# Two-layer RWKV and mixture-of-experts network on one core: dense experts' first units moved into the first layer's last tile, its first tiles reordered, and the low halves of the squared relus subtracted on VectorE

## The reference, cut to what matters

```python
h = W_E[x] * 16
xn = layernorm(layernorm(h))                   # h is normalized twice
w, k, v, r = -exp(xn @ Ww.T), xn @ Wk.T, xn @ Wv.T, sigmoid(xn @ Wr.T)
# along each sequence: num = decay*num + exp(w+k)*v ; den = decay*den + exp(w+k)
x2 = x1 + (r * num / (den + 1e-8)) @ Wo.T
kk = square(relu(layernorm(x2) @ Wkey.T))      # 1024 wide
h = h + x2 + sigmoid(layernorm(x2) @ Wrec.T) * (kk @ Wval.T)
xf = layernorm(h)
logits = xf @ Wrt + br                         # router of 8 experts, top 2, softmax
h = h + sum_e weight_e * (gelu(xf @ W1[e] + b1[e]) @ W2[e] + b2[e])   # 8 dense experts, 256 -> 1024 -> 256
# then the second layer: WKV attention, causal attention, 4 experts
```

## Time and profile before

| | |
|---|---|
| median of 3 runs | 3027.48 us (3025.65 to 3029.61) |
| profiled execution, its own time | 3026.94 us |
| its span in the profile | 3024.9 us |
| PE (TensorE matmul) busy | 2725.5 us, 90% |
| VectorE (DVE) busy | 1906.0 us, 63% |
| ScalarE (ACT) busy | 1842.6 us, 61% |
| GpSimd (POOL) busy | 391.2 us, 13% |
| mean granted TensorE clock | 0.979 |

### The profile page before, as it was taken

The page is one execution under the profiler, slowest core; times in us unless marked ns, Lnnn a source line. Parts: engine busy times, 40 slices in busy tenths (PEclk is TensorE's granted clock), DMA queues, the critical chain, the costliest instruction groups (busy, mean ns, idle before and its releaser), DMA issues.

```text
span 3024.9 us, 55642 instructions
## 1 busy us (share of the span) xinstructions
PE 2725.5 (90%) x22016; PEld 1819.0 (60%) x22016; DVE 1906.0 (63%) x4021; ACT 1842.6 (61%) x2877; POOL 391.2 (13%) x462
## 2 busy tenths in 40 slices
PE   3989877998999999999999999999999998998889
PEld 1555554565665566657665766566656665663665
DVE  5767736757666665666566665666565657656664
ACT  3666645655766566666665766576657665665644
POOL 5666530000000000100010001000100010011000
PEclk8999988999999999999999999999999999999999
DMA  1000008832122222222222222222222221110002
GB/s 64 22 21 20 21 13 309 286 119 78 63 74 96 77 74 71 88 80 76 76 89 86 76 67 89 81 76 76 90 80 76 74 77 63 71 57 27 27 24 79
DMA packets 59742, 235.66 MB, mean 78 GB/s; under 512 B 6585, under 2 KB 25073, under 8 KB 40689
## 3 DMA queue, kind: packets, MB, share of 16 engines
q1 hardware_dynamic: 57968, 228.14, 21.6%
q0 software_dynamic: 1536, 4.20, 0.5%
HBM read 200.57 MB, written 31.72 MB: 77 GB/s over the span
## 4 chain that ended last, share of the span: by engine, by line
PE 51%; DVE 16%; ACT 10%; issue 4%; DMA 2%; POOL 2%; SPq 0%; ACTq 0%; DVEq 0%
PE c_up L2303 15%; PE c_down L2318 14%; PE c_up L2053 8%; ACT c_g L1571 3%; PE c_down L2375 2%; DVE c_lo L1957 2%; DMA c_room<-in_WB 2%; PE c_front L2062 1%; PE c_front L2075 1%; DVE c_mx L1821 1%; PE c_front L2187 1%; DVE c_room L1739 1%; PE c_front L2053 1%; PE c_front L2191 1%; DVE h L1947 1%
## 5 line engine op out<-in xcount | busy, mean ns | idle before, releaser
L2303 PE MATMUL c_up<-c_xT,c_ring 128*128 128x512 bf16 x3072 | 743.2, 380 | 32.3 <-ACT c_g L1571 13.4
L2318 PE MATMUL c_down<-c_ring,c_hi 128*128 128x256 bf16 x4096 | 699.9, 274 | 21.4 <-DVE c_lo L1957 8.9
L1957 DVE TENSOR_TENSOR c_lo<-c_g,c_hi 128x512 bf16<-128x512 f32 x720 | 481.5, 685 | 308.3 <-ACT c_hi L1573 291.2
L1571 ACT ACTIVATE c_g<-c_up,b 128x512 f32<-128x512 f32 x512 | 350.3, 684 | 473.6 <-PE c_up L2303 458.2
L2318 PE MATMUL c_down<-c_ring,c_lo 128*128 128x256 bf16 x2048 | 560.3, 274 | 0.0
L2318 PEld LDWEIGHTS c_down<-c_ring,c_hi 128*128 128x128 bf16 x4096 | 394.2, 98 | 145.9 <-issue 30.0
L2303 PEld LDWEIGHTS c_up<-c_xT,c_ring 128*128 128x128 bf16 x3072 | 292.6, 98 | 312.6 <-ACT c_g L1571 21.8
L1573 ACT ACTIVATE c_hi<-c_g 128x512 bf16<-128x512 f32 x688 | 433.3, 630 | 21.7
L1393 POOL TENSOR_TENSOR c_xlo<-c_room,c_xhi 128x512 bf16<-128x512 f32 x48 | 54.8, 1157 | 1504.4 <-ACT c_xhi L1418 1504.4
L2318 PEld LDWEIGHTS c_down<-c_ring,c_lo 128*128 128x128 bf16 x2048 | 201.0, 98 | 24.0
L1571 ACT ACTIVATE c_g<-c_up 128x512 f32<-128x512 f32 x176 | 104.7, 595 | 179.7 <-PE c_up L2053 178.3
(11 more groups left out here) (353 smaller groups left out, 5018.6 us busy)
## 6 DMA issues: line engine op xcount, KB each, us to landing
c_ring<-kept_dense SPq DMA_DIRECT2D x112, 1024.0 KB, 4.8
c_ring<-kept_experts SPq DMA_DIRECT2D x63, 512.0 KB, 3.4
c_room<-in_WB SPq DMA_DIRECT2D x16, 1024.0 KB, 6.9
kept_dense<-c_ring SPq DMA_DIRECT2D x16, 1024.0 KB, 4.8
c_ring<-kept_experts SPq DMA_DIRECT2D x28, 384.0 KB, 3.4
kept_experts<-c_room SPq DMA_DIRECT2D x9, 512.0 KB, 4.5
c_xT<-kept_xT SPq DMA_DIRECT2D x8, 512.0 KB, 5.1
out<-h SPq DMA_DIRECT2D x8, 512.0 KB, 6.9
```

The lines of the kernel that those rows point to most:

```text
L1571: act.activation(g[:, h % 4, :], ub[n % 2][:, :], ACT.Gelu, bias=bias).then_inc(g_ready.sem, 1)
L1957: dve.tensor_tensor(lo14[:, a, :], g[:, h % 4, :], hi14[:, a, :], ALU.subtract).then_inc(lo_ready.sem, 1)
L2303: last = pe.matmul(ub[n % 2][:, :], r[:, wp, o + q * P:o + (q + 1) * P], xT[:, xp, q, :], start=(m == 0 and q == 0), stop=(m == 2 and q == ...
L2318: m = pe.matmul(bank, (hi14, lo14)[xp][:, a, s * P:(s + 1) * P], r[:, wp, o + KC * P:o + CHUNK], start=(k == 0 and n == 0 and s % 2 == 0), ...
```

## The change

Five things:

- **The experts' start moves into `phase_a`.** In the last tiles SP loads the first four weight pieces and tile 0's `xT`, ACT and VectorE split the first two (`wp0`, `wp1`), and PE and ACT do the units U0 to U4 (gelu of U0 to U3) (`up`, `up4`, order `ORDER_END`). For that, buffers of the two blocks are shared (`ring01`, `room0`, `xT`, `g`, `ub`). The block no longer waits for the last store to land; SP waits for it at the start of the next block. The router's maxima and softmax and some memsets go to later units (`ROUTER_AT`), so the exponential now stands between gelus.
- **The low halves of the squared relus** go from POOL to VectorE, one token later (`kl0` to `kl3`).
- **The order of the steady tiles**: `bx` after `c1`; `e0` on VectorE between the statistics of the second norm and its application (`c0n`).
- **The order of the first tiles** (`ORDER_FILL`), the constants `lc` last; POOL's masks go to the second block.
- **The loop over tiles 1 to 5** (`Fori`) is written out.

```diff
-ORDER_A = ("c0 bx b0 e0 d0 dx ag k0 b1 e1 c1 sm z0 k1 b2 c2 tr z0x c3 zx0 a0 c4 a0p z1 z1x c5 zx1 an l0 l1 c6 a1 c6p "
-           "dr lc l2 l3 l4 l5 l6").split()
+ORDER_A = ("c0 b0 e0 c0n d0 dx ag k0 b1 e1 c1 bx sm z0 k1 b2 c2 tr kl0 z0x c3 zx0 kl1 a0 c4 kl2 a0p "
+           "z1 z1x c5 zx1 an kl3 wp0 l0 l1 c6 a1 c6p wp1 dr l2 l3 l4 l5 l6 lc").split()
+ORDER_END = "up d0 dx up4 dr".split()
+ORDER_FILL = "ag bx b0 e0 a0 k0 b1 e1 a0p z0 k1 an b2 tr a1 z0x zx0 z1 z1x zx1".split()
...
-        fb = [x.enter_context(nc.psum_tensor(f"a_front{k}", [P, TT], F32)) for k in range(4)]
+        fb = c.ub + [x.enter_context(nc.psum_tensor(f"a_front{k}", [P, TT], F32)) for k in (2, 3)]
...
+        emb, xn = (c.ring01[0][:, j, :].bitcast(F32) for j in range(2))
+        x2, xn2 = (c.ring01[1][:, j, :].bitcast(F32) for j in range(2))
+        x1 = c.g[:, 0:2, :].rearrange("p k n -> p (k n)")
+        yf = c.g[:, 2:4, :]
...
+        ek, ev, num, den = (c.room0[:, j * KC * TT:(j + 1) * KC * TT].rearrange("p (k n) -> p k n", k=KC) for j in range(4))
+        tr = c.xT[:, :, :, :].rearrange("p a k n -> p (a k n)").bitcast(F32).rearrange("p (k n) -> p k n", k=KC)
...
-        def run(eng, A, B, C, D, L):
+        def run(eng, A, B, C, D, L, ahead):
 
             braid(A(0), L)
-            braid(A(1), B(0))
+            braid(A(1), B(0), order=ORDER_FILL)
             braid(A(2), B(1), C(0))
-            with eng.Fori(1, TILES - 2) as t:
+            for t in range(1, TILES - 2):
                 braid(A(t + 2), B(t + 1), C(t), D(t - 1))
             braid(B(TILES - 1), C(TILES - 2), D(TILES - 3))
-            braid(C(TILES - 1), D(TILES - 2))
-            braid(D(TILES - 1))
+            braid(C(TILES - 1), D(TILES - 2), ahead)
+            braid(D(TILES - 1), ahead, order=ORDER_END)
 
         block = x.enter_context(nc.Block())
 
...
-            with sp.Fori(0, TILES) as t:
+            for t in range(TILES):
+                if t == TILES - 2:
+
+                    sp.wait_ge(z_ready.sem, z_ready.at(TILES - 1))
+                    sp.wait_ge(xm_kept.sem, xm_kept.at(t, 0))
+                    sp.dma_start(c.xT[:, :, :, :], c.xd[0, :, :, :, :]).then_inc(c.xT_in.sem, 16)
+                    for p in range(2):
+                        sp.dma_start(c.room0[:, p * PIECE:(p + 1) * PIECE], c.i["WB"][p, :, :]).then_inc(c.loaded[p].sem, 16)
+                if t == TILES - 1:
+                    for q in range(2):
+                        sp.wait_ge(c.split, 2 * (q + 1))
+                        sp.dma_start(c.room0[:, q * PIECE:(q + 1) * PIECE], c.i["WB"][q + 2, :, :]
+                                     ).then_inc(c.loaded[q].sem, 16)
                 sp.wait_ge(xm_lo.sem, xm_lo.at(t))
                 for j, part in enumerate((c.xT_hi, c.xT_lo)):
                     sp.dma_start(c.xd[bass.ds(t, 1), :, j, :, :].rearrange("g p k n -> (g p) k n"),
                                  part[:, :].rearrange("p (k n) -> p k n", k=KC)[:, :, bass.ds(t * TT, TT)]
                                  ).then_inc(xm_kept.sem, 16)
             sp.wait_ge(s_b2, 16 * len(BIAS))
-            sp.wait_ge(xm_kept.sem, 32 * TILES)
-
         @block.gpsimd
         def _(pool):
...
-                def low(*ks):
-                    def f():
-                        for k in ks:
-                            pool.wait_ge(sq_ready.sem, sq_ready.at(t, k + 1))
-                            pool.wait_ge(k_hi.sem, k_hi.at(t, k + 1))
-                            pool.tensor_tensor(klo[:, k, :], sq[:, k % 2, :], khi[:, k, :],
-                                               ALU.subtract).then_inc(k_lo.sem, 1)
-                    return f
-
                 def b6():
                     rstd(bmv, brs, b_var, b_rstd, b_pool, t, 1)
-                return {"c0": b0, "c1": b1, "c2": low(0, 1), "sm": summed, "c3": low(2, 3), "c4": low(4, 5), "c5": low(6, 7),
-                        "c6p": b6}
-            run(pool, stage_a, stage_b, stage_c, lambda t: {}, {"lc": masks})
+                return {"c0": b0, "c1": b1, "sm": summed, "c6p": b6}
...
+            def first_pieces(q):
+                def f():
+                    act.wait_ge(c.loaded[q].sem, 16)
+                    if q == 1:
+                        act.wait_ge(h_sum.sem, h_sum.at(TILES - 1))
+                    for half in range(2):
+                        cols = slice(half * PIECE // 2, (half + 1) * PIECE // 2)
+                        act.activation(c.ring01[q][:, 0, cols], c.room0[:, q * PIECE + half * PIECE // 2:
+                                                                        q * PIECE + (half + 1) * PIECE // 2],
+                                       ACT.Copy).then_inc(c.split_hi, 1)
+                return f
+
+            def gelus(*us):
+                def f():
+                    for u in us:
+                        act.wait_ge(c.up_ps, u + 1)
+                        act.wait_ge(h_sum.sem, h_sum.at(TILES - 1))
+                        act.wait_ge(y_lo.sem, y_lo.at(TILES - 1))
+                        act.activation(c.g[:, u, :], c.ub[u % 2][:, :], ACT.Gelu,
+                                       bias=c.b1[:, u:u + 1]).then_inc(c.g_ready, 1)
+                return f
+            run(act, stage_a, stage_b, stage_c, stage_d, {"l%d" % k: high(k) for k in range(NCH)},
+                {"wp0": first_pieces(0), "wp1": first_pieces(1), "up": gelus(*range(AHEAD))})
 
...
-                    norm(S, lambda s: x2[:, s * D:(s + 1) * D], xn2, bst, bmv, brs, b_var, b_rstd, t, 0, xn2_ready)
+                    norm_stats(S, lambda s: x2[:, s * D:(s + 1) * D], bst, bmv, b_var)
+
+                def b0n():
+                    norm_apply(S, lambda s: x2[:, s * D:(s + 1) * D], xn2, bmv, brs, b_rstd, t, 0, xn2_ready)
...
+                def low(*ks):
+                    def f():
+                        for k in ks:
+                            dve.wait_ge(sq_ready.sem, sq_ready.at(t, k + 1))
+                            dve.wait_ge(k_hi.sem, k_hi.at(t, k + 1))
+                            dve.tensor_tensor(klo[:, k, :], sq[:, k % 2, :], khi[:, k, :],
+                                              ALU.subtract).then_inc(k_lo.sem, 1)
+                    return f
+                return {"c0": b0, "c0n": b0n, "kl0": low(0, 1), "kl1": low(2, 3), "kl2": low(4, 5), "kl3": low(6, 7), "c6": b6}
...
-            run(dve, stage_a, stage_b, stage_c, stage_d, {"lc": constants, **{"l%d" % k: low(k) for k in range(NCH)}})
+
+            def first_pieces(q):
+                def f():
+                    dve.wait_ge(c.loaded[q].sem, 16)
+                    for half in range(2):
+                        cols = slice(half * PIECE // 2, (half + 1) * PIECE // 2)
+                        dve.wait_ge(c.split_hi, 2 * q + half + 1)
+                        dve.tensor_tensor(c.ring01[q][:, 1, cols], c.room0[:, q * PIECE + half * PIECE // 2:
+                                                                           q * PIECE + (half + 1) * PIECE // 2],
+                                          c.ring01[q][:, 0, cols], ALU.subtract).then_inc(c.split, 1)
+                return f
+            run(dve, stage_a, stage_b, stage_c, stage_d, {"lc": constants, **{"l%d" % k: low(k) for k in range(NCH)}},
+                {"wp0": first_pieces(0), "wp1": first_pieces(1)})
 
...
+            def first_units(*us):
+                def f():
+                    pe.wait_ge(tr_ready.sem, tr_ready.at(TILES - 1))
+                    pe.wait_ge(c.xT_in.sem, c.xT_in.at(0))
+                    pe.wait_ge(c.split, 2 * (us[-1] // 4 + 1))
+                    for u in us:
+                        if u >= 2:
+                            pe.wait_ge(c.g_ready, u - 1)
+                        for m, (wp, xp) in enumerate(PARTS):
+                            for q in range(KC):
+                                last = pe.matmul(c.ub[u % 2][:, :],
+                                                 c.ring01[u // 4][:, wp, u % 4 * CHUNK + q * P:
+                                                                  u % 4 * CHUNK + (q + 1) * P],
+                                                 c.xT[:, xp, q, :], start=(m == 0 and q == 0),
+                                                 stop=(m == 2 and q == KC - 1))
+                        last.then_inc(c.up_ps, 1)
+                return f
+            run(pe, stage_a, stage_b, stage_c, stage_d, {}, {"up": first_units(*range(AHEAD)), "up4": first_units(AHEAD)})
 
...
+ROUTER_AT = {("D", 0): "mx", ("D", 2): "sx", ("D", 30): "ms"}
...
-SPLITS, _at = {}, 0
-for _q, (_kind, _p) in enumerate(FIRST_LOADS[1:], 1):
+SPLITS, _at = {}, 2
+for _q, (_kind, _p) in enumerate(FIRST_LOADS[2:], 2):
...
+            if u in ROUTER_AT:
+                ORDER_0.append(ROUTER_AT[u])
...
+            sp.wait_ge(c.xm_kept, 32 * TILES)
...
-                sp.dma_start(staged[q % 2][:, 0:n], src).then_inc(loaded[q % 2].sem, 16)
-                if q == 0:
-                    load_x(0)
+                if q >= 4:
```

(8 more changed lines are left out.)

115 lines of the change are left out of this document (62 added, 53 removed).

## The result

| | before | after |
|---|---|---|
| median | 3028.47 us (6 runs) | 3014.84 us (3013.03 to 3017.20, 6 runs) |
| profiled execution, its own time | 3026.94 us | 3015.76 us |
| span | 3024.9 us | 3014.0 us |

What follows compares the result with a forecast made beforehand. PE, busy 90% of the span, was taken as the bound, so only its waits could shrink. Switch -17.9, start -6.8, steady tiles +6.0, tile behind the loop +4.3 sum to -14.4: 3013.0 us by the median, range 2998 to 3026.

Steps and rivals of the forecast that it cites:

- The switch: Second block's start and first expert loads: the whole train of loads moves 17.1 us earlier; -17.9 us together.
- Table loads: ACT, exponential now between gelus: three loads instead of one, 1.28 us each, costed at nothing; 2.6 us without DMA cover.
- The start: First layer's start: earlier splits, gathers and statistics let L608 begin at 67.5, not 74.30; -6.8 us.
- The steady tiles: Loop tiles and the one before: `down(0)` starts 1.3 us later, one half-clock stretch; +1.0 a tile, +6.0 us.
- The tile behind the loop: Tile after the loop, 44.32 us before: takes 46.6, plus 2.0 for a half-clock stretch; +4.3 us.
- The written-out loop: Loop over tiles 1 to 5: costed at nothing, as its branch lies where PE is ahead of VectorE.
- No half clock at all (1): Rival, steady tiles: no half-clock stretch, -4.8 for six tiles, +2.3 behind the loop: 3000 us; chance 0.26.
- Two stretches a tile (2): Rival, steady tiles: two half-clock stretches each, +18.6 and +6.5: 3028 us, no change; chance 0.14.
- The train of loads did move (3): Rival, switch: the loads' train doesn't move as a whole, only PE's first wait goes: 3018.5 us; chance 0.08.
- Slower (4): Rival, seven tiles: subtractions take all VectorE's slack, 4.8 us a tile, 33.6 against 24.7 gained: 3036.5 us; chance 0.06.

Runs made afterwards that it cites:

- masks_late: Against the changed kernel, GpSimd builds the second layer's masks after all weight pieces are split, not at the second block's start: 3012.22 us.
- both1: Changed kernel with block 0's subtraction between the second scans, second ratio before block 3's subtraction, masks as in masks_late, memsets behind D28: 2991.64 us.
- old_fill: Against the changed kernel, the first tiles' order is the old one, with the constants ahead of the third weight split: 3018.13 us.
- masks_start: Against the changed kernel, GpSimd builds the masks in the first layer's first tile again, not at the second block's start: 3020.93 us.
- klo_pool: Against the changed kernel, the eight low halves of the squared relus are back on GpSimd at their former places: 3003.61 us.

## Why the prediction was right, and where not

*The switch (-17.9, measured -9.9).* The mechanism was right: the train of loads moved, and taking the early start out costs 10.9. The size was off by 8.0, in three places. First, of VectorE's list I counted all operations but not what ran beside them: POOL's masks held two of them for 3.6 us, so the sixth load came 15.8 us behind the block's start and not 12; masks_late gives that 12. Counted from the block's start the load moved 13.3 us and not 17.1: 3.8 are missing. (That it stands 16.8 us earlier in all is also the first layer's doing, which ends 4.0 earlier.) Second, the block's start itself: forecast 0.8 nearer to the last mixing, it is 0.6 further from it (SP's first row, 452.66, is 16.1 behind L648 at 436.54; before, 456.14 was 15.6 behind 440.58). That is 1.4: what leaving out the wait for the last store gave, the splits ahead of the block's end took back. Third, between the sixth load and the end of tile 0 another 2.8 were lost: the memsets of 3.3 us, which the change moved into the loads' stretch, stood ahead of a sum that PE waits for (4.77), 2.3 by both1, and 0.5 stay open.

*Table loads (0).* Both are there, 1.28 us each, ACT's next row follows the second at once (466.94), and no wait of PE names them. The 2.66 us for a switch, which the prediction took from the Trainium skill ("ScalarE: Activation LUTs", What ACT_TABLE_LOAD costs), is not what this trace shows: there is no gap of a drain, neither ahead of a load nor behind it.

*The start (-6.8, measured -8.3).* Near in size, wrong in cause, so the size is luck. The prediction let VectorE's splits hold POOL's index copy, and the new order remove that. old_fill and masks_start show that it was mostly the masks, which the sum didn't have at all: they stood ahead of the copy for 9 us and slowed VectorE's small operations (the first `kw` is at 37.77, against 44.16 before).

*The steady tiles (+6.0, measured +0.2).* The step was right to a tenth or three: PE waits 2.59 and 1.48 us (predicted 2.3 and 1.5), and klo_pool shows that the move to VectorE costs 11.5 us. Mis-sized was the tile, forecast at +1.0 in all six. The tile ahead of the loop got 1.9 shorter (from the first residual to the first mixing 38.54 us, before 40.46): its clock is 1.00, where before it fell behind a wait of 2.22 (0.55 over 3.80 us). The five loop tiles got 2.1 longer together, not 5.0. I had taken every tile before for the one of 47.47 that I read, and one of the five has no stretch at half clock (45.81), so they average 47.05; after they average 47.47 and not 48.5. A tile of the kernel after takes 46.55 without a stretch, 47.97 to 48.23 with one behind the wait of 2.59: the stretch costs 1.6 and not 2.0. The first loop tile has one too, but elsewhere: behind the wait of 1.96 for `xT_lo` (0.52 over 3.50 us). It costs that tile nothing, for PE, being later, then waits 0.92 ahead of the first block and not 2.59. What PE loses ahead of a wait that another engine ends comes out of that wait.

The clock fell behind the wait of 2.59 us in four of five tiles (0.58 over 4.10 us, so 1.2 GHz and not 2.4 for most of that), behind that of 1.48 in none of seven. So a mean over few tiles mixes the work with how often the clock fell, and tiles are to be compared like with like: on POOL (klo_pool) a tile takes 45.08 to 45.17 without a stretch and 46.65 to 46.82 with one, which makes the subtractions' move 1.4 us a tile, and the reordering's own gain 0.7 (45.81 before). That is 7 of klo_pool's 11.5 us; the tile behind the loop gives 4.8, and by the trace the tile ahead of the loop takes back what fewer stretches give.

*The tile behind the loop (+4.3, measured +4.1).* Right; with the subtractions on POOL it takes 43.65 again.

*The written-out loop (0).* The branch costs nothing that shows; but in the new order the loop would have cost 16 us through another engine. So this term of the sum, at nothing, was the one furthest off, and the new order's forecast holds only with the loop written out. That an edit of its own costs nothing does not make it worth nothing beside others. What it does in the kernel before was not tried; there `ylo` starts ahead of L578, which takes 1.20.

*The rivals.* No half clock at all (1) came in one loop tile of five. Two stretches a tile (2) did not come, since 1.48 us was not followed by one. The train of loads did move (3). Slower (4) asked for 4.8 us a tile from eight subtractions; klo_pool puts it at 1.4, or 1.7 with the stretches (47.5 against 45.8): most of their time went into VectorE's idle time ahead of L648, 8.08 us before and 2.43 after.

## What to carry to other kernels

When work moves between GpSimd and VectorE, list what each runs beside the other at its new place: a row that takes far longer than the same row elsewhere (here 1.7 to 12 times) is the sign, and a shift of 0.7 us on the other engine can decide it. A short operation for which TensorE waits is placed by when its input is ready, not behind the longer chain that happens to stand there: one subtraction moved ahead of a pair of scans gave 18 us here. Parts of a change that only keep others harmless show nothing until they are taken out of the finished version.

## What the runs showed that I had not expected

A VectorE row of 0.43 us (L606) took 1.20 where GpSimd's operation had begun 0.42 us before it, and 5.08 where it began 0.22 us behind, with two more queued. The Trainium skill ("SBUF — State Buffer", SBUF: two separate sides) has the shared ports as an exclusive lock, held for a whole instruction, on which the loser blocks. By that rule the row waits for as many of GpSimd's operations as get the lock ahead of it; its end (284.50) lies 0.29 us behind the last of them (284.21), which agrees. The same section gives the lock to the one that starts first; by the rows' starts that was VectorE (279.42 against 279.64), and it lost. GpSimd's last gather row still ran then (278.66 to 279.61); whether that is the reason, no run here shows.

The same wait, 1.96 to 1.98 us, was followed by a stretch at half clock in four of five loop tiles before, but in two of klo_pool's five (0.58 over 4.00 us in one of them; in the other three the tile's clock is 1.00): a stretch at half clock is read from the windows of several tiles, not of one.
